# A token shift made by DMAs inside SBUF in place of two transpositions and a copy, and a new order of the steps

## The reference, cut to what matters

```
def shift_token(t):
    t1, t2 = jnp.split(t, 2, axis=-1)
    t2 = jnp.pad(t2, ((0, 0), (1, 0), (0, 0)))[:, :-1]
    return jnp.concatenate([t1, t2], axis=-1)

def _layer(x, ...):
    ...
    x = x + o @ wo
    h = shift_token(x)
    mu = h.mean(-1, keepdims=True)
    var = h.var(-1, keepdims=True)
    h = (h - mu) / jnp.sqrt(var + 1e-05) * lg + lb
    h = h @ w1 + b1
    a, g = jnp.split(h, 2, axis=-1)
    h = a * jax.nn.gelu(g, approximate=False)
    return x + h @ w2 + b2
```

## Time and profile before

| | |
|---|---|
| median of 3 runs | 5209.54 us (5208.2 to 5211.27) |
| the profiled execution | 5208.83 us |
| its span, first to last instruction | 5207.0 us, so 1.8 us lie around it |
| granted TensorE clock over the span | 0.997 of full speed |
| PE busy | 5089.8 us, 98% of the span |
| PE weight loads | 4142.8 us, 80% |
| DVE busy | 3371.8 us, 65% |
| ACT busy | 2933.1 us, 56% |
| POOL busy | 2614.3 us, 50% |
| DMA | 280.81 MB, 54 GB/s over the span |

### The profile page before, as it was taken

The page is one execution under the profiler, slowest core; times in us unless marked ns, Lnnn a source line. Parts: engine busy times, 40 slices in busy tenths (PEclk is TensorE's granted clock), DMA queues, the critical chain, the costliest instruction groups (busy, mean ns, idle before and its releaser), DMA issues.

```text
span 5207.0 us, 177128 instructions
## 1 busy us (share of the span) xinstructions
PE 5089.8 (98%) x72856; PEld 4142.8 (80%) x72856; DVE 3371.8 (65%) x8313; ACT 2933.1 (56%) x7591; POOL 2614.3 (50%) x2308
## 2 busy tenths in 40 slices
PE   7999999999999999999999999999999999999998
PEld 5887888878888788887888887788777887878787
DVE  6656676666766667666676665766657676566764
ACT  4556555555555565555655556555556555565554
POOL 5445555455544456444464543645436455455543
PEclk9999999999999999999999999999999999999999
DMA  2211111111111211111121111201211112111110
GB/s 82 98 69 54 59 36 66 46 65 48 39 62 47 71 42 39 63 61 56 42 67 36 62 55 46 65 31 62 66 41 60 43 51 67 46 54 59 35 50 17
DMA packets 51392, 280.81 MB, mean 54 GB/s; under 512 B 5280, under 2 KB 22688, under 8 KB 33696
## 3 DMA queue, kind: packets, MB, share of 16 engines
q1 hardware_dynamic: 39840, 252.69, 13.2%
q0 software_dynamic: 10752, 16.78, 1.7%
HBM read 249.01 MB, written 28.84 MB: 53 GB/s over the span
## 4 chain that ended last, share of the span: by engine, by line
PE 96%; issue 1%; DVE 1%; ACT 1%; POOL 1%; SPq 0%; DMA 0%; POOLq 0%; ACTq 0%; DVEq 0%
PE bank_M L729 11%; PE bank_S L712 10%; PE bank_S L714 9%; PE bank_S L713 9%; PE bank_F L660 7%; PE bank_F L661 6%; PE bank_F L662 6%; PE bank_F L916 6%; PE bank_M L748 5%; PE bank_F L806 5%; PE bank_M L837 5%; PE bank_F L849 4%; PE bank_F L821 4%; PE bank_M L756 2%; PE bank_F L788 1%
## 5 line engine op out<-in xcount | busy, mean ns | idle before, releaser
L1497 POOL TENSOR_TENSOR q_lo<-q_mix,q_hi 128x512 fp32r<-128x512 f32 x512 | 668.4, 1306 | 1233.6 <-ACT q_hi L981 1233.6
L994 ACT ACTIVATE probs<-bank_S,neg_max 128x512 f32<-128x512 f32 x1024 | 700.9, 685 | 778.8 <-DVE neg_max L1227 688.7
L1227 DVE TENSOR_REDUCE neg_max<-bank_S 128x1 f32<-128x512 f32 x1024 | 696.2, 683 | 303.3 <-PE bank_S L714 300.0
L712 PE MATMUL bank_S<-k_hi,q_lo 128*128 128x512 f32 x2048 | 876.8, 428 | 7.2 <-POOL q_lo L1497 5.1
L714 PE MATMUL bank_S<-k_hi,q_hi 128*128 128x512 f32 x2048 | 805.7, 393 | 0.0
L713 PE MATMUL bank_S<-k_lo,q_hi 128*128 128x512 f32 x2048 | 805.0, 393 | 0.0
L729 PEld LDWEIGHTS bank_M<-mixer_n,probs 64*64 64x64 f32 x32768 | 528.1, 135 | 188.9 <-issue 165.8
L1492 POOL TENSOR_TENSOR q_mix<-q_rope,w_pre 128x256 f32<-128x256 f32 x1024 | 631.6, 638 | 52.2 <-POOL q_lo L1497 0.9
L1523 POOL TENSOR_TENSOR l_probs<-l_probs,l_inv 128x1024 f32<-128x1024 f32 (+1 forms) x256 | 429.2, 1682 | 396.1 <-DVE l_inv L1330 396.1
L729 PE MATMUL bank_M<-mixer_n,probs 64*64 64x64 f32 x32768 | 600.4, 222 | 14.0 <-issue 9.9
L1053 ACT ACTIVATE l_probs<-l_probs,l_least 128x256 f32<-128x256 f32 (+1 forms) x1024 | 480.5, 472 | 185.2 <-DVE l_least L1310 183.6
(11 more groups left out here) (142 smaller groups left out, 10173.8 us busy)
## 6 DMA issues: line engine op xcount, KB each, us to landing
w_qkv_hi<-split_qkv SPq DMA_DIRECT2D x30, 1536.0 KB, 6.7
w_qkv_lo<-split_qkv SPq DMA_DIRECT2D x30, 1536.0 KB, 6.3
w_hi<-split SPq DMA_DIRECT2D x30, 1408.0 KB, 6.1
w_lo<-split SPq DMA_DIRECT2D x30, 1408.0 KB, 8.3
w<-in_w SPq DMA_DIRECT2D x32, 768.0 KB, 4.2
w_o<-in_w_o SPq DMA_DIRECT2D x32, 512.0 KB, 5.2
x_in<-in_x POOLq DMA_DIRECT2D x16, 512.0 KB, 3.8
out_y<-in_x SPq DMA_DIRECT2D x16, 512.0 KB, 7.7
```

Of the source, the lines that this page charges most:

```text
L712: mm(bank[k][:], q_lo[q], k_hi[:, s, :], start=(s == 0), stop=False)
L994: fn(probs[:, n % PB, :], bank[k][:], ACT.Exp, bias=neg_max[:, n % 2:n % 2 + 1], accum_out=row_sum[:, n % 4:n % 4 + 1]).then_inc(emptied[k ...
L1227: v.tensor_reduce(neg_max[:, n % 2:n % 2 + 1], bank[k][:], AX.X, ALU.max, negate=True)\
L1497: g.tensor_tensor(q_lo[:, c % QB], q_mix[:], q_hi[:, c % QB].bitcast(F32), ALU.subtract)\
```

## The change

The two transposing steps, ACT's copy and the tile `midT` go. A tile `shifted` of [128, 4, 128] is filled by DMAs from SP. After DVE has written window t of `x_mid`, one DMA moves partitions 0 to 126 of its upper half to partitions 1 to 127 of `shifted[t]`, and a second one, except after window 3, moves partition 127 to partition 0 of window t + 1. Partition 0 of window 0 is zeroed once. All seven DMAs of a layer raise one semaphore, `shift_done`, for whose full count DVE waits at the head of the step `mid_stats` (the former `shift_turn`). The bias step of POOL, with the load of the next input, is now a step of its own, `mid_bias`. `h_scale` reads `shifted` instead of F1, window by window. F0 and F1 are no longer used between the last `local_scores` and `up`. All three order tables are new.

SP's part of `out_proj`:

```
 def out_proj(step, l, t):
+    if t == 0 and now.past(l):
+        sp.wait_ge(h_ready, now.at(h_ready, TW * l))
+    sp.wait_ge(emptied["F3"], now.fill(step, "F3"))
+    sp.dma_start(shifted[1:P, t, :], x_mid[0:P - 1, t, P:D]).then_inc(shift_done, 16)
+    if t < TW - 1:
+        sp.dma_start(shifted[0:1, t + 1, :], x_mid[P - 1:P, t, P:D]).then_inc(shift_done, 16)
     if t == TW - 1 and not last(l):
         sp.wait_ge(filled["F3"], now.fill(step, "F3"))
         sp.dma_start(w_o[:], a["w_o"][(l + 1) % LAYERS]).then_inc(w_o_loaded, 16)
```

PE's two steps, which go:

```
-def half_turn(step, l):
-    pe.wait_ge(emptied["F3"], now.fill(("out_proj", l, TW - 1), "F3"))
...
-        last = turn(bank["F0"][:, t * P:(t + 1) * P], x_mid[:, t, P:D], ident[:])
...
-def shift_turn(step, l):
-    pe.wait_ge(emptied["F0"], now.fill(("half_turn", l), "F0"))
...
-        last = turn(bank["F1"][:, t * P:(t + 1) * P], midT[:, t * P:(t + 1) * P], ident[:])
```

ACT's copy, which goes:

```
-def half_turn(step, l):
...
-    fn(midT[:, 1:N + 1], bank["F0"][:], ACT.Copy).then_inc(emptied["F0"], 1)
```

DVE's statistics:

```
-def shift_turn(step, l):
-    dve.wait_ge(filled["F1"], now.fill(step, "F1"))
+def mid_stats(step, l):
+    dve.wait_ge(shift_done, now.at(shift_done, SHIFTS * (l + 1)))
     dve.wait_ge(emptied["F3"], now.fill(("out_proj", l, TW - 1), "F3"))
...
-        v.bn_stats(stats[:, t, 1, :], bank["F1"][:, t * P:(t + 1) * P]).then_inc(stats_done, 1)
+        v.bn_stats(stats[:, t, 1, :], shifted[:, t, :]).then_inc(stats_done, 1)
```

A piece of `ORDER` in layer 0, before and after:

```
-out_proj.0.3 half_turn.0 mix.11 shift_turn.0 expand.14 scores.24 part.14 project.0 h_scale.0 scores.25 values.2
+mixers.10 out_proj.0.2 local_values.0.6 p_turn.0.7 scores.22 local_values.0.7 scores.23 out_proj.0.3 mix.10 mixers.11
+scores.24 store mid_stats.0 mix.11 scores.25 project.0 mid_bias.0 mixers.12 part.14 values.2 h_scale.0 scores.26
```

The new order at the same place in layer 1:

```
+p_turn.1.6 weigh.1.7 scores.50 scores.51 mixers.25 out_proj.1.2 expand.28 scores.52 part.28 mix.25 scores.53
+local_values.1.6 p_turn.1.7 scores.54 expand.29 local_values.1.7 mixers.26 part.29 scores.55 mixers.27 expand.30
+mix.26 out_proj.1.3 part.30 scores.56 mix.27 mid_stats.1 scores.57 project.2 scores.58 mixers.28 values.6 h_scale.1
```

## The result

| | before | the change |
|---|---|---|
| median of the runs beside each other | 5210.41 us (5208.2 to 5213.36, 4 runs) | 5366.24 us (5363.57 to 5370.87, 4 runs) |
| span of the profiled execution | 5207.0 us | 5365.7 us |
| PE busy | 5089.8 us | 5109.0 us |
| PE idle (span less busy) | 117.2 us | 256.7 us |
| granted TensorE clock | 0.997 | 0.981 |

The ratio is 1.03, 95% interval 1.0282 to 1.0317: slower, and by 156 us where 49 were forecast. The span grew by 158.7 us: 139.5 us is idle time of PE and 19.2 us is busy time, although the transpositions are gone. First the page of the change, busy times.

What follows compares the result with a forecast made beforehand. PE, busy 98% of the span, was taken as the bound. 5208.8 us minus 62.6 of removed work and waits plus 112 of stall for the shift gave 5258 us; range 5162 to 5340, this case alone 5220 to 5340.

Steps and rivals of the forecast that it cites:

- The sign: Whole kernel: the change makes it slower; all slower outcomes together had chance 0.65.
- the mechanism that was put first: DVE's wait at `mid_stats`: 127-row shifts run on one DMA engine, queued behind loads, stalling PE; chance 0.62.
- the 62.6 us that were to go: PE: 29 us transpositions, 8.3 us wait of the first one, 25.3 us wait for the next input, all removed.
- the 112 us of the sum: PE idle before `values.2` and `values.6`: 5.1 us in layer 0, 1.9 in layer 1, over 16 batches.
- PE work that goes: Two steps of four transpositions per layer vanish from PE: 1.82 us per batch, 29 us in 16.
- a new wait of PE at a place that the new order alone has made: Listed last among signs that the forecast is wrong; no size given.
- The landing at T+12.1: Layer 0, window 3's shift: lands 12.1 us after T, the issue of `w_1_lo`, behind loads and window 2's shift.
- the upper end, 5.0 us: A 127-row shift alone: 5.0 us on one engine, against 1.8 if dealt over sixteen.
- The first rival: Shift rows dealt over all engines, landing with `w_1_lo` at T+8.3: 5168 us, not slower; chance 0.24.
- the third rival: No queue: loads and shifts share engines by turns; stalls 61 us, 5207 us, no change; chance 0.08.
- The second rival: Small packets between SBUF tiles cost much more than 27 ns; at twice that 5421 us; chance 0.06.
- Edits that I cost at nothing: ACT's copy, DVE reading SBUF, POOL's later bias, SP's waits: nothing; without DVE slack, scaling a few tenths per layer.

Runs made afterwards that it cites:

- e1: The change without the shift DMAs and the wait for them, DVE reading a tile of zeros; 5208.81 us, 1.0003 of the kernel before.
- e6: The kernel before, transpositions kept, with only the batch's tail ordered as in the new order; 5192.11 us, 0.9969 of the kernel before.
- e2: The change with the output store moved right behind the step that makes its data; 5338.97 us, 1.0252 of the kernel before.
- e13: e9 with the 127 rows of a shift in one DMA again; 5258.17 us, 1.0098 of the kernel before.
- e3: The change with each 127-row shift cut into two DMAs, of 112 and 15 rows; 5268.19 us, 1.0121 of the kernel before.
- e9: e8 with the load of `w_qkv_lo` moved further, behind `h_scale`; 5188.1 us, 0.9964 of the kernel before.
- e4: The change with both the 112 and 15 row pieces and the early store; 5251.24 us, 1.009 of the kernel before.
- e7: e2 with the loads `w_qkv_lo` and `w_1_lo` issued behind the layer's last shift; 5257.25 us, 1.0088 of the kernel before.
- e12: e9 with `scores.25` ahead of `project.0`, and `h_scale` and `scores.26` between `project.0` and `values.2`; 5249.07 us, 1.0083 of the kernel before.
- e14: e12 with GpSimd's `mid_bias.0` taken behind `h_turn.0`; 5206.51 us, 0.9996 of the kernel before.
- e8: The change with pieces, early store, both loads behind the shift, and `scores.25` between `project.0` and `values.2`; 5220.52 us, 1.0022 of the kernel before.

## Why the prediction failed

The sign was right and the mechanism that was put first was the one at work; the size was off by 108 us. Two steps failed: the 62.6 us that were to go did not, and the stall was dearer than the 112 us of the sum. The spans and busy times of the kernel before, of e1 and of the change split the miss:

| | forecast | measured |
|---|---|---|
| before to e1 (order without shift), PE busy | -29 | -13.1 |
| before to e1, PE idle | -33.6 | +10.5 |
| e1 to the change (the shift), PE idle | +112 | +129.0 |
| e1 to the change, PE busy | 0 | +32.3 |

The four differences, 16, 44, 17 and 32 us, add up to the 109 us by which the span was missed.

1. **The gain of 62.6 us did not come: e1's interval allows at most 3 of it.** The term "PE work that goes" had 29 us; busy PE fell by 13.1 in e1. The wait of the first transposition did go, and 23.8 of the 25.3 us for xT_lo left their line, but e6 shows the tail to be worth 16 to 18 us of time. Against that stand 35.6 us of a new wait that the new order makes by itself. The prediction named this possibility last ("a new wait of PE at a place that the new order alone has made") and priced it at nothing. A third of it could have been read: the list of steps has `scores.25 project.0 ... values.2`, and I let `values.2` begin the moment `project.0` ends, while `s_tok` is read and written by DVE between them. The earlier trace rows price that at 0.35 us of wait and 0.42 of addition, a third of the 2.4 us of e1. The rest is the store, which the new order has moved from early in the batch to just ahead of `mid_stats.0` and which reads the tile that the addition writes. The prediction left the store out altogether.

2. **The stall of 112 us was 129 us of idle PE.** In layer 0 I had 5.1 us and the trace has 9.45. The landing at T+12.1 was T+16.5, 4.4 us more. The sum also ended with DVE's copy, though DVE does a maximum and the addition before `values.2` may begin, as I had counted in layer 1: 1.06 us more, 17 us in 16 batches. And PE came 1.1 us later than I thought (T+10.8). Of the 4.4 us the store is 2.5: e2, without it, lands at T+14.0. It is worth 27 us. The rest is open in part. In e2 the engines reach full share only from T-1.0 and are busy to between T+7 and T+8, where I had T-1.8 and T+5.7 from the kernel before. In layer 1 I had a landing at T+10.1 and 1.9 us; the trace has T+10.7 and 1.1 to 2.2. That part of the sum held.

3. **The rows on one engine: right.** I took the upper end, 5.0 us for a shift alone; e13 measures 5.5 from issue to DVE's release, with a DMA share of one engine. The rule that the prediction cites from the Trainium skill, "DMA: Bandwidth & Descriptors", section "Why a DMA increments its semaphore by 16 and not by 1", holds here: with 112 and 15 rows the time falls by 98 us (e3), by 70 with nothing ahead (e13 and e9). The first rival falls for the kernel as it was written and tells what it would be with one line changed. Its time, 5168, was too low by the 60 us of point 1, the store (17 us, e3 to e4) and the queue: e3 has 5268.

4. **The loads ahead hold the shift up: the third rival is out.** It had the landing of layer 0 at T+8.9. Loads behind the shift instead of ahead gave 82 us (e2 to e7), which agrees with the ring order that the Trainium skill states in "Queues, rings and completion order" of the same page. The second rival, dear packets, is out by the 5.5 us; it needs 8.4.

5. **The half clock had no term.** PE's long waits let the clock fall, and the work behind them begins at 0.50. By windows of 1 us, PE's busy time at that clock is 25 us before, 49 in e1 and 115 in the change. Work at half takes about twice as long, so half of the difference is lost: some 33 us from e1 to the change, where busy PE grew by 32.3. This is an estimate, but it leaves nothing of the growth over.

6. **"Edits that I cost at nothing"** had DVE reading SBUF. Before, four of the eight scaling instructions read PSUM and the eight took 2.94 us (1136.25 to 1139.19), although a subtraction of GpSimd (1138.13 to 1139.41) ran beside the four that read PSUM. In the change the eight take 5.7 (1172.51 to 1178.19), in e12 5.4, in e14 3.55. The forecast allowed "a few tenths per layer"; where GpSimd is at work it is up to 2.7 us. In the change PE hardly waits for it (2.3 us for `shared` in all); in e12 the maximum behind it comes late.

What stays open: why PE's busy time falls less than the transpositions took. In e1 the half clock accounts for 12 of the missing 16 us. In e9 it doesn't: 5074.3 us, against 5083.4 in e6 with its transpositions, where 29 lie between by my count and the clock makes up some 3. So the mechanism has shown no gain of its own: the best kernel with it (e9, 0.9964) and the best with the transpositions (e6, 0.9969) can't be told apart, and both are faster than the kernel before, by 0.3 to 0.4%, and than the change.

## What to carry to other kernels

A DMA of 127 rows ran on one engine of sixteen, was slow by itself (70 us of the whole) and worse behind loads (88 us): where a number of rows like this one comes up, cut it into a multiple of 16 and a rest, and issue it ahead of the bulk loads. Other numbers of rows were not tried here. Before a step is moved, read off for every neighbour pair in the new order what one engine hands to another between them, and which DMA issues of all queues fall into the same stretch. Try the parts of a reordering alone: here the tail by itself (e6) gave what the whole order gave with the pieces, the early store, the gap and both loads moved (e9). Put a price on the half clock behind PE's long waits: here it is some 33 of the 157 us that the shift costs.

## What was unexpected of the hardware

- SP's issue of the load of `w_o` took 7.29 us when a 127-row shift and two loads stood in the queue ahead of it, and the two loads' own issues 0.52 and 0.33; in e3, with pieces, the same issue took 0.54.
- PE paused for 2.19 us in the midst of a step that waited for nothing, with three loads in a row on the DMA engines (e8); the place of one load decided over 32 us. The cause is not shown.
- A scaling instruction of DVE on SBUF operands took 1.97 us instead of 0.33 beside GpSimd's issue of a load and a subtraction (the change and e12); four that read PSUM took 1.36 us together beside the same subtraction (before).
